# Rows in blocks of four, the last y set copied by DVE and ACT, and half of the padded weight copies moved to ACT, in a one-core attention kernel

## The reference, cut to what matters

```python
x = x + conv(_ln_c(x))        # _ln_c: normalized over the last axis j
# conv:
q, k, v = Wq·y, Wk·y, Wv·y                        # over channels c
qk  = einsum('ncij,nchj->nihj', q, k) / d
qrq = einsum('ncij,chi->nihj', q, rq) / d ; krk the same with k, rk
weight = softmax(qk + Gq*qrq + Gk*krk, axis=3)    # over j
out = einsum('nihj,nchj->ncij', weight, Gv1*v) + einsum('nihj,chi->ncij', weight, Gv2*rv)
```

## Time and profile before

| | |
|---|---|
| median of 3 runs | 140.41 us (140.3 to 140.84) |
| the profiled execution | 140.75 us, of which 139.0 us are the span of the page |
| busy | PE 104.0 us (75%), PEld 76.2, DVE 92.7, ACT 70.5, POOL 66.7 |
| chain that ended last | PE 29%, POOL 19%, DVE 18%, ACT 13%, issue 8%, SP's queue 5%, DMA 5% |
| mean granted TensorE clock | 0.972 |
| DMAs into spread4 | 16 for y and 16 for the weights, 128 KB each, 2.3 to 2.6 us to landing |

### The profile page before, as it was taken

The page is one execution under the profiler, slowest core; times in us unless marked ns, Lnnn a source line. Parts: engine busy times, 40 slices in busy tenths (PEclk is TensorE's granted clock), DMA queues, the critical chain, the costliest instruction groups (busy, mean ns, idle before and its releaser), DMA issues.

```text
span 139.0 us, 4748 instructions
## 1 busy us (share of the span) xinstructions
PE 104.0 (75%) x2078; PEld 76.2 (55%) x2080; DVE 92.7 (67%) x145; ACT 70.5 (51%) x154; POOL 66.7 (48%) x77
## 2 busy tenths in 40 slices
PE   0694995995689999990999599495886979999100
PEld 0331331284689999880989499441322438999100
DVE  5798927334030196897771069399999787889991
ACT  7957884940542456154600232424553399999200
POOL 8975855970000037628500099999965000007940
PEclk9999999999999999999599999999999999999985
DMA  4892660269100000058085000000000000000767
GB/s 146 257 282 19 151 150 1 55 136 224 50 5 5 5 5 2 5 121 188 5 190 122 5 0 5 5 5 0 0 0 0 0 0 0 5 0 17 203 185 201
DMA packets 8800, 9.56 MB, mean 69 GB/s; under 512 B 2316, under 2 KB 6412, under 8 KB 8780
## 3 DMA queue, kind: packets, MB, share of 16 engines
q1 hardware_dynamic: 8780, 9.26, 26.7%
HBM read 2.97 MB, written 2.10 MB: 36 GB/s over the span
## 4 chain that ended last, share of the span: by engine, by line
PE 29%; POOL 19%; DVE 18%; ACT 13%; issue 8%; SPq 5%; DMA 5%; POOLq 0%; ACTq 0%
PE ps L1006 9%; PE ps L1021 7%; POOL y_tile L428 6%; ACT warm L656 5%; PE ps L1042 5%; SPq L289 4%; POOL u_tile L422 4%; DVE xin L347 4%; POOL y_tile L434 4%; PE ps L1054 3%; DMA xin<-in_x_dram 3%; DVE y_tile L353 3%; PE ps L1030 3%; DVE stat L693 3%; ACT v_tile L656 2%
## 5 line engine op out<-in xcount | busy, mean ns | idle before, releaser
L403 POOL TENSOR_TENSOR att_tile<-att_tile,soft 128x1024 f32<-128x1024 f32 x4 | 7.7, 1935 | 23.9 <-DVE soft L754 23.9
L353 POOL TENSOR_TENSOR y_tile<-xin,u_tile 128x256 f32<-128x256 f32 (+1 forms) x7 | 7.1, 1046 | 20.8 <-DVE xin L347 20.8
L1006 PE MATMUL ps<-spread,u_tile 128*32 128x64 f32 x512 | 12.6, 252 | 3.9 <-issue 2.2
L1042 PE MATMUL ps<-spread,rv_t 128*32 128x128 f32 x256 | 12.0, 360 | 3.6 <-issue 3.6
L1006 PEld LDWEIGHTS ps<-spread,u_tile 128*32 128x32 f32 x512 | 12.1, 193 | 4.4 <-issue 4.4
L1042 PEld LDWEIGHTS ps<-spread,rv_t 128*32 128x32 f32 x256 | 10.9, 132 | 4.3 <-issue 3.9
L903 DVE TENSOR_SCALAR ps<-att_tile,bnv 128x512 f32<-128x512 f32 x15 | 11.0, 807 | 1.6 <-ACT warm L656 1.6
L1054 PE MATMUL ps<-spread,v_tile 128*32 128x64 f32 x512 | 9.1, 223 | 3.7 <-issue 3.7
L765 DVE TENSOR_TENSOR u_tile<-ps,xin 128x512 f32<-128x512 f32 x8 | 5.4, 687 | 8.5 <-PE ps L1042 8.2
L1114 PE MATMUL ps<-blank 128*128 128x512 bf16 x40 | 9.8, 379 | 1.5 <-DVE u_tile L796 1.3
L1054 PEld LDWEIGHTS ps<-spread,v_tile 128*32 128x32 f32 x512 | 8.5, 109 | 4.3 <-issue 4.1
(11 more groups left out here) (109 smaller groups left out, 232.4 us busy)
## 6 DMA issues: line engine op xcount, KB each, us to landing
spread<-rel_tile SPq DMA_DIRECT2D x16, 128.0 KB, 2.6
out_dram<-y_tile SPq DMA_DIRECT2D x8, 256.0 KB, 2.4
xin<-in_x_dram SPq DMA_DIRECT2D x3, 512.0 KB, 4.9
spread<-att_tile SPq DMA_DIRECT2D x12, 128.0 KB, 2.4
xin<-in_x_dram SPq DMA_DIRECT2D x2, 256.0 KB, 2.8
spread<-u_tile SPq DMA_DIRECT2D x4, 128.0 KB, 2.3
att_tile<-in_L_conv_rv_dram SPq DMA_DIRECT2D x4, 128.0 KB, 2.6
att_tile<-in_L_conv_rq_dram SPq DMA_DIRECT2D x1, 128.0 KB, 6.3
```

The lines of the kernel that those rows point to most:

```text
L353: return eng.tensor_tensor(result[:, :, rows, :], back[:, at:at + P * k].rearrange("p (q i j) -> p q i j", q=Q, i=k), x2[:, :, rows, :], A ...
L1006: return nc.tensor.matmul(ps[group(q), first + j // 8, at:at + G * HALF].rearrange("p (g i) -> p g i", g=G), u[:, q, :, j], y_bd[:, q, :, ...
L1042: ins = nc.tensor.matmul(bank(4 + n % 4)[group(g), P * k:P * (k + 1)].rearrange("p (q jp t) -> p q jp t", q=Q, t=RUN), rv_t[:, ROWS * n + ...
```

## The change

Within an image the elements are now stored as (b, j, k): block b of four rows, column j, row k of the four. `scores` and `weighted_sums` then read runs of four elements, 512 bytes from run to run, and `relative_scores` and `relative_values` read 128 elements that are 16 bytes apart. Turning y and weighing a chunk are one instruction each. Set 3 of y is no longer turned and transferred: DVE copies images 0 to 2 and ACT image 3 straight into `spread4`. Of the weights' chunks ACT copies sets q = 0 and 1, and SP transfers 2 and 3. ACT's order changes: both copies of the first half stand behind `score_exp(1)`, `score_exp(2)` stands between `value_out` 5 and 6, and the copies of the second half stand behind the table load.

```diff
-        y_bd = spread4[:, :, :, :].rearrange("p q g (b jp i t) -> p q g b jp i t", b=2, i=HALF, t=RUN)
-        att_bd = spread4[:, :, :, :].rearrange("p g q (b jp i t) -> p g q b jp i t", b=2, i=HALF, t=RUN)
+        y_bd = spread4[:, :, :, :].rearrange("p q g (b j k) -> p q g b j k", b=PIECES4, j=C)
+        att_bd = spread4[:, :, :, :].rearrange("p g q (b j k) -> p g q b j k", b=PIECES4, j=C)
...
-        turned_att = rel_tile[:, :].rearrange("p (x g jp i t) -> p x g i jp t", x=CHUNKS, g=2, i=HALF, t=RUN)
+        turned_att = rel_tile[:, :].rearrange("p (x m j k) -> p x m k j", x=CHUNKS, j=C, k=ROWS)
...
+        COPIED = 2
...
+        def y_block(q, g):
+            return turned(spread4[group(g), q, g, :])
+
+        def y_rows(q, g):
+            return by_blocks(y[group(g), q, :, :])
...
             def spread_att(n):
...
-                for q in range(Q):
+                for q in range(COPIED, Q):
                     sp.dma_start(spread4[group(q), gs, q, BANK * half:BANK * (half + 1)],
...
             spread_y(2)
-            spread_y(3)
...
             def weigh(n):
                 pool.wait_ge(S["weight_recip"], n + 1)
-                for g in range(2):
-                    nc.gpsimd.tensor_tensor(turned_att[:, n, g, :, :, :], by_pairs(att[:, n, g, :, :]), recip_of(2 * n + g), ALU.mult
-                                            ).then_inc(S["weights"], 1)
+                nc.gpsimd.tensor_tensor(turned_att[:, n, :, :, :], by_blocks(att_m[:, n, :, :]), recip_of(n), ALU.mult
+                                        ).then_inc(S["weights"], 1)
...
             def turn_y(q):
...
-                for b in range(2):
-                    nc.scalar.copy(in_pairs(turned_y[q])[:, b], by_pairs(y[:, q, HALF * b:HALF * (b + 1), :])).then_inc(S["y_turned_act"], 1)
+                nc.scalar.copy(turned(turned_y[q]), by_blocks(y[:, q, :, :])).then_inc(S["y_turned_act"], 1)
...
-            turn_y(3)
+            wait_y(act, 3)
+            act.wait_ge(S["spread_zero3"], 2)
+            nc.scalar.copy(y_block(3, 3), y_rows(3, 3)).then_inc(S["y_copied_act"], 1)
...
+            def copy_att(n):
+                half, gs = n // 2, slice(2 * (n % 2), 2 * (n % 2) + 2)
+                wait_weights(act, n)
+                act.wait_ge(S["score_b_high" if half else "score_a"], 1)
+                act.wait_ge(S["rel_product"], PIECES4 // 2 * (half + 1))
+                for q in range(COPIED):
+                    nc.scalar.copy(spread4[group(q), gs, q, BANK * half:BANK * (half + 1)],
+                                   rel_tile[group(q), IMG * n:IMG * (n + 1)].rearrange("p (g k) -> p g k", g=2)
+                                   ).then_inc(S["att_copied"], 1)
+
             score_exp(0)
             score_exp(1)
+            copy_att(0)
+            copy_att(1)
             value_out(4)
             value_out(5)
+            score_exp(2)
             value_out(6)
             value_out(7)
-            score_exp(2)
             score_exp(3)
             nc.scalar.preload_act_table(ACT.Sqrt)
+            copy_att(2)
+            copy_att(3)
...
+            dve.wait_ge(S["y_ready_dve"], 3)
+            dve.wait_ge(S["spread_zero3"], 2)
+            for g in range(G - 1):
+                nc.vector.tensor_copy(y_block(3, g), y_rows(3, g)).then_inc(S["y_copied_dve"], 1)
...
-                                        u[:, q, :, j], y_bd[:, q, :, half, j // RUN, :, j % RUN],
+                                        u[:, q, :, j], y_bd[:, q, :, rows_of(half), j, :],
...
-                                               r_fac[:, ROWS * n + k, :], y_bd[:, q, :, n // 4, :, ROWS * (n % 4) + k, :],
+                                               r_fac[:, ROWS * n + k, :], y_bd[:, q, :, n, :, k],
...
-                                               rv_t[:, ROWS * n + k, :], att_bd[:, g, :, half, :, row + k, :],
+                                               rv_t[:, ROWS * n + k, :], att_bd[:, g, :, n, :, k],
...
-                                               v_t[:, j, g, :], att_bd[:, g, :, half, j // RUN, :, j % RUN],
+                                               v_t[:, j, g, :], att_bd[:, g, :, rows_of(half), j, :],
...
-            for q in range(Q):
+            for q in range(Q - 1):
                 pe.wait_ge(S[f"y_in{q}"], 16 * G)
+            pe.wait_ge(S["y_copied_dve"], G - 1)
+            pe.wait_ge(S["y_copied_act"], 1)
...
-            pe.wait_ge(S["att_in0"], 16 * Q * 2)
+            pe.wait_ge(S["att_in0"], 16 * (Q - COPIED) * 2)
+            pe.wait_ge(S["att_copied"], COPIED * 2)
```

More of the change, by code:

```diff
@@ L20 @@
 CHUNKS = 4
-RUN = 2
 WARM = 9
@@ L160, in wait_y, with turned, by_blocks, rows_of @@
                 eng.wait_ge(S["y_ready_dve"], {0: 2, 3: 3}[q])
-        def in_pairs(t):
-            return t.rearrange("p (b jp i t) -> p b i jp t", b=2, i=HALF, t=RUN)
-        def by_pairs(t):
-            return t.rearrange("p i (jp t) -> p i jp t", t=RUN)
+        def turned(t):
+            return t.rearrange("p (b j k) -> p b k j", b=PIECES4, j=C)
+        def by_blocks(t):
+            return t.rearrange("p (b k) j -> p b k j", k=ROWS)
+        def y_block(q, g):
+            return turned(spread4[group(g), q, g, :])
+        def y_rows(q, g):
+            return by_blocks(y[group(g), q, :, :])
         def recip_of(n):
-            return soft[:, 1, n // 2, HALF * (n % 2):HALF * (n % 2 + 1)].unsqueeze(2).unsqueeze(3).broadcast_to([P, HALF, C // RUN, RUN])
+            return soft[:, 1, n, :].rearrange("p (b k) -> p b k", k=ROWS).unsqueeze(3).broadcast_to([P, PIECES4, ROWS, C])
+        def rows_of(half):
+            return slice(PIECES4 // 2 * half, PIECES4 // 2 * (half + 1))
         def wait_weights(eng, n):
-            eng.wait_ge(S["weights_dve" if n % 2 else "weights"], 2 * (n // 2 + 1))
+            eng.wait_ge(S["weights_dve" if n % 2 else "weights"], n // 2 + 1)
         def unit(t, k):
@@ L769, in weigh @@
                 dve.wait_ge(S["weight_recip"], n + 1)
-                for g in range(2):
-                    nc.vector.tensor_tensor(turned_att[:, n, g, :, :, :], by_pairs(att[:, n, g, :, :]), recip_of(2 * n + g), ALU.mult
-                                            ).then_inc(S["weights_dve"], 1)
+                nc.vector.tensor_tensor(turned_att[:, n, :, :, :], by_blocks(att_m[:, n, :, :]), recip_of(n), ALU.mult
+                                        ).then_inc(S["weights_dve"], 1)
             score_add(0)
@@ L1005, in score @@
                 at = G * HALF * (j % 8)
-                return nc.tensor.matmul(ps[group(q), first + j // 8, at:at + G * HALF].rearrange("p (g i) -> p g i", g=G),
-                                        u[:, q, :, j], y_bd[:, q, :, half, j // RUN, :, j % RUN],
+                return nc.tensor.matmul(ps[group(q), first + j // 8, at:at + G * HALF].rearrange("p (g b k) -> p g b k", g=G, k=ROWS),
+                                        u[:, q, :, j], y_bd[:, q, :, rows_of(half), j, :],
                                         start=True, stop=True)
@@ L1020, in relative_scores @@
                     for q in range(Q):
-                        ins = nc.tensor.matmul(side_bank(n)[group(q), P * k:P * (k + 1)].rearrange("p (g jp t) -> p g jp t", g=G, t=RUN),
-                                               r_fac[:, ROWS * n + k, :], y_bd[:, q, :, n // 4, :, ROWS * (n % 4) + k, :],
+                        ins = nc.tensor.matmul(side_bank(n)[group(q), P * k:P * (k + 1)].rearrange("p (g j) -> p g j", g=G),
+                                               r_fac[:, ROWS * n + k, :], y_bd[:, q, :, n, :, k],
                                                start=True, stop=True)
@@ L1034, in relative_values @@
             def relative_values(n):
-                half, row = n // 4, ROWS * (n % 4)
                 if n < 4:
@@ L1041, in relative_values @@
                     for g in range(G):
-                        ins = nc.tensor.matmul(bank(4 + n % 4)[group(g), P * k:P * (k + 1)].rearrange("p (q jp t) -> p q jp t", q=Q, t=RUN),
-                                               rv_t[:, ROWS * n + k, :], att_bd[:, g, :, half, :, row + k, :],
+                        ins = nc.tensor.matmul(bank(4 + n % 4)[group(g), P * k:P * (k + 1)].rearrange("p (q j) -> p q j", q=Q),
+                                               rv_t[:, ROWS * n + k, :], att_bd[:, g, :, n, :, k],
                                                start=True, stop=True)
@@ L1053, in weighted_sums @@
                     for g in range(G):
-                        ins = nc.tensor.matmul(ps[group(g), first + j // 8, at:at + Q * HALF].rearrange("p (q i) -> p q i", q=Q),
-                                               v_t[:, j, g, :], att_bd[:, g, :, half, j // RUN, :, j % RUN],
+                        ins = nc.tensor.matmul(ps[group(g), first + j // 8, at:at + Q * HALF].rearrange("p (q b k) -> p q b k", q=Q, k=ROWS),
+                                               v_t[:, j, g, :], att_bd[:, g, :, rows_of(half), j, :],
```

(3 more changed lines are left out.)

10 lines of the change are left out of this document (4 added, 6 removed).

## The result

The changed kernel takes 144.88 us (median of 4 runs, 144.44 to 146.69), the kernel before 140.62 us beside it: a ratio of 1.029, interval 1.024 to 1.034. It is slower, where I had forecast 139.0 and "faster"; the time lies inside the range. Its profiled execution took 144.57 us with a span of 142.7 (before: 140.75, span 139.0), so 3.7 us of span have to be found.

What follows compares the result with a forecast made beforehand. PE was taken to lead the chain (29%), with two holes waiting on copies. Weighted_sums(0) ending 1.4 us earlier gave 140.75 - 1.4 = 139.35; the profiled run lay 0.34 above the median, so 139.0 us, range 132.3 to 146.5.

Steps and rivals of the forecast that it cites:

- Part 1: Set 3 of y copied by DVE and ACT: scores start at 32.4 instead of 34.00, -1.6 us; doubled writes, +1 us.
- Part 3: One weigh instruction per chunk: POOL -0.2 us, DVE's two become one for less; a doubled 16-byte write, +1.9.
- a rival at 140.5: Gain and loss cancel: relative matmuls at 57 to 60 ns, or a doubled write in copies or weigh; chance 0.12.
- Part 2: Blocks of four: relative matmuls at 55 ns, relative scores +3.9 us; runs of four in scores and sums gain nothing.
- At 57 to 58 ns nothing is left of the gain: Relative matmuls: at this spacing the forecast's gain, -1.4 us at the end of weighted_sums(0), would be used up.
- the slope of 0.38: 384 relative matmuls on the path: 0.38 us of kernel time per ns of their spacing.
- The collision: Rival: the four streams of relative matmuls collide, 79 ns instead of 55, +9 us, 147.5; chance 0.27.
- no extra cost: Rival: relative matmuls' 16-byte steps cost no more than the pairs; 134.2 us at 40 ns; chance 0.28.
- Part 4: Weights' copies by ACT, 1.05 us each, SP two issues per chunk instead of four; relative values start at 65.0, not 66.32.
- In before 64: SP's four issues of weights' transfers, at 0.8 with 2.4 to land, are in before 64, ahead of relative values at 65.0.
- Second half: I cost nothing: Second half's relative values take 7.0 us for 5.3 or so, but end as now or 0.6 earlier; no cost.

Runs made afterwards that it cites:

- e10: Changed kernel with weighs, ACT's turns and direct copies of y writing contiguously, so results come out for other elements: 141.73 us, ratio 1.016.
- e4: Changed kernel with DVE's copies of y held back until POOL's copies into w_bd are done: 143.51 us.
- e1: Kernel before with the new layout and single weigh alone; set 3 of y and all weights still go by transfers: 147.55 us.
- e12: Changed kernel with weighted_sums(0) held back until ACT's last copy of weights: 147.50 us, ratio 1.055.
- e8: Changed kernel with relative matmuls reading runs of 32 contiguous elements, so they multiply other elements than they should: 137.54 us, ratio 0.977.
- e2: Kernel before, in pairs, with only half of the weights' copies made by ACT: 137.77 us.
- e5: Kernel before, in pairs, with both sets of copies: y's set 3 by DVE and ACT, half of the weights by ACT: 134.54 us, ratio 0.959.
- e6: Kernel before with runs of four instead of pairs and no copies moved; scores and sums read lone elements 16 bytes apart: 143.59 us, ratio 1.023.
- e9: Changed kernel with both weighs, POOL's and DVE's, writing contiguously, so results come out for other elements: 143.50 us, ratio 1.032.

## Why the prediction was wrong

The forecast's own chain against the changed kernel's profile, in us:

| event | predicted | measured | late by |
|---|---|---|---|
| scores start | 32.4 | 34.24 | 1.8 |
| relative scores end | 54.6 | 57.17 | 2.6 |
| exp(0) | 55.4 | 57.72 | 2.3 |
| weights(0) ready | 60.2 | 63.17 | 3.0 |
| relative values start | 65.0 | 68.43 | 3.4 |
| relative values end | 72.0 | 76.0 | 4.0 |
| sums(0) end | 77.45 | 81.47 | 4.0 |
| profiled time | 139.35 | 144.57 | 5.2 |

**The step that failed first is the 16-byte write, in Parts 1 and 3.** I had both its bounds, no penalty and double, and took none, although I had just argued the double for the read from the ACT row of 2065 ns. ACT's turns and copies do double (2.04 against 1.03) and DVE's weigh takes 1.99 against 1.23. DVE's copies of y were not the trouble in themselves: 1.10 us each, where I had 1.2. It was ACT's turn, ahead of the projections. Part 1's "doubled ... +1 us" was too small as well, because of a neighbour that I had not named: POOL's copies into w_bd stand on PE's way to the early values and run beside DVE's copies of y. Together they are the first 1.8 us of the table, but for the 0.36 of the start: with plain writes the scores come 7.80 us behind the first turn, the forecast's 32.4 - 24.60 (e10); with DVE out of POOL's way alone 8.33 (e4); as changed 9.28.

The writes aren't the whole miss. Taken away (e10) they bring the change from +4.3 to +1.7 us, still not the -1.4 of the forecast. Doubled, they stood in the prediction at +1 in Part 1 and +1.9 in Part 3, and as a rival at 140.5; both together would have made 141.9, over the border to "slower". The rest I look for in the terms below.

**Part 3** said -0.2 for POOL and a gain for DVE. POOL's weigh takes 2.49 and 2.06 instead of 1.93; DVE's takes 1.8 and 2.2 us more than before. Of the first, 1.99 is the step without neighbours (e1), and the rest I put down to the 1.0 us that it shares with POOL's weigh: where they share 0.9 it takes 2.97 (e1, without ACT's copies) and 2.94 (e12), where they don't overlap 2.35 (e8); that is argued, as e8 changed PE's reading too. Of the second, 1.6 us come from the sums (e12). On the path this is less than it looks. POOL's 0.6 counts in full. DVE's first weigh ends at 65.33, when SP has just finished the issues of the chunk before it (65.14), so it delays the transfers by 0.2 us; the second delays them so that PE waits 0.36.

**Part 2's relative matmuls were right**: 55 ns forecast, 57.7 and 56.4 measured, by the double that two kinds of rows gave. The 2.7 and 1.4 ns above 55 are 0.9 us over 384 matmuls. "At 57 to 58 ns nothing is left of the gain" doesn't follow from the slope of 0.38, by which the 1.4 us are used up at 58.7; at 57 to 58 some 0.3 to 0.6 are left, too little to measure. (The collision's sum is off too: 139.0 and 9 make 148, not 147.5. Nothing hangs on it.) The rival of colliding streams is wrong (388 to 432 ns), and so is "no extra cost". Scores and sums as runs of four: worth nothing, as forecast; they run at 3.00 and 2.94 us per block against 3.07 and 3.04, and keep their pauses. Why the sums hinder others now and not in pairs I had no row for.

**Part 4** was right for ACT: four copies of 1.07 before value_out, and the wait of 3.65 us is 0.69 in e2. In the changed kernel they end at 67.47, 3.1 late, all inherited from above. It was wrong for SP, and that changes which wait ends last. "In before 64" allows 3.8 us from the first weights on, but four issues at 0.8 and 2.4 to land are 5.6 by the same sentence, which makes 65.8, later than the 65.0 that I took from ACT. Measured from the first weights to the relative values it is 5.3 (63.17 to 68.43), 6.1 in e5 and 5.7 in e10 (60.41 to 66.06), and each time PE's wait ends with a transfer. In the changed kernel that costs 0.4 us over ACT's path, on which value_out(4) is done at about 68.0.

**"Second half: I cost nothing"** was wrong by about 1 us: its relative values take 7.58 us, where they took 5.66 before, and DVE's first t_sum (L830), for which POOL's L434 waits, stands behind two residual steps that follow them. That is the step from 2.6 us at the sums to 3.5 at POOL.

With the parts taken singly: layout +7.7 (e1), both copies -5.5 (e5), which add up to +2.2, while the change gives +4.3. The missing 2.1 are hindrances that need both. Two are seen: DVE's copies beside POOL's, 0.95 at the start of the scores and 0.6 in the time (e4, for whose time no interval is given), and sums beside ACT's copies, 1.4 us over the four (2.93 + 2.67 against 2.12 + 2.11 in e12). How much of the time the second takes stays open, as e12's wait costs more than it frees.

**The chances.** I gave 0.28 to slower, nearly all of it to colliding reads, which didn't happen. That the time lies inside the range is therefore luck: the outcome came in the main from a term for which I held both ends and took the favourable one in two parts, while the spacing, on which I had hung most, came out right.

## What to carry to other kernels

When a layout moves a step to one side, price it for everyone who reads and for everyone who writes. Lone 4-byte elements 16 bytes apart cost here about twice on PE and ACT and 1.6 times on DVE, and turning the view round only gives them to another reader (e6). Pairs, in which no one has lone elements at that step, were the better compromise: e5 keeps them and moves only the copies, for 134.54 us. And when work moves to an engine that is idle, look at what its neighbours do in those microseconds, small copies included.

## What the runs showed of the hardware that was not expected

*POOL and DVE copies take turns.* POOL's four copies of 96 elements into w_bd take 4.13 us while DVE's copies of y run beside them, 1.10 each; 2.95 beside plain copies of 0.70 (e10); 2.10 beside copies of 0.48 (e5); and 1.75 where DVE waits (e4). By their median, one takes 1.05, 0.66 and 0.40 us beside these, each time a little less than a copy by DVE, and 0.27 alone. The Trainium skill (SBUF — State Buffer, Who interferes with whom) says that a DVE copy in a two-port mode holds the pair of ports shared with GpSimd for the whole instruction; if DVE's copies run in that mode, which no row shows, each small copy waits out one of them, and these durations agree.

*Sums on PE slow ACT and DVE.* ACT's copy of 1024 elements takes 1.05 us and beside the sums of the changed kernel up to 1.86; DVE's weigh 2.00 and 3.61 (e12). The same section of the Trainium skill says "PE and ACT never wait on anyone"; here the measurement decides against it for ACT. With the weighs plain, four copies of which the last run beside sums still took 4.76 (e9) and 5.14 us (e10). In e2 and e5 the sums, in pairs, ran beside such copies with no loss (4.30 and 4.33 for four); in e8 ACT's copies lost little (4.38), but POOL's weigh took 3.60 us beside the first sums, instead of 2.24 for its first one. What makes the difference was not tried.

*The relative read doesn't feel the clock*: 56.4 ns with nearly half of the stretch at 1.2 GHz, 57.7 at 2.4 GHz; 128 of them took 7.57 us at a mean granted clock of 0.78 and 7.58 at 1.00 (e12). In pairs, at a mean clock of 0.73, 128 matmuls took 6.38 us, against 5.6 for 126 at full clock in e5.

*Lone elements cost PE by the element*: 57 ns for 128 columns and 30 for 64 (e6's sums) are 0.45 and 0.47 each, against 27.5 and 14.8 to 16.0 without the step.
